# Attention and mixture of experts in one program: q and k in two float16 parts, two heads on the array's two 64-row halves

## The reference

```python
qkv = x @ W_qkv                               # (16,1024,256) @ (256,768)
q, k, v = split(qkv); q, k = rope(q, k)       # 16 heads of 16
att = einsum('bhtd,bhsd->bhts', q, k) / 4 + causal_mask
w = softmax(att)
x = layernorm(x + einsum('bhts,bhsd->bhtd', w, v) @ W_o)
gate = softmax(x @ Wg + bg); top 2 of 8, normalised
y = sum over experts of gate_e * (x @ We[e].T + be[e])
out = layernorm(x + y)
```

## Time and profile before

| | |
|---|---|
| three runs, median | 3236.32 us (3235.18 to 3238.13) |
| span of the profiled execution | 3236.3 us |
| PE busy | 3109.0 us, 96% of the span |
| DVE busy | 2677.5 us, 83% |
| ACT busy | 1884.1 us, 58% |
| POOL busy | 1200.8 us, 37% |
| chain that ended last | PE 84%, DVE 8%, issue 3%, ACT 2% |

### The profile page before, as it was taken

One profiled execution on the slowest core, in us unless ns is written; L12 is line 12 of the kernel. 1 busy time (PEld: TensorE's weight loads), 2 busy tenths in 40 slices (PEclk: granted clock), 3 DMA queues, 4 the chain that ended last, 5 costly groups with the idle time before them and its releaser, 6 DMA issues.

```text
span 3236.3 us, 58547 instructions
## 1 busy us (share of the span) xinstructions
PE 3109.0 (96%) x18752; PEld 1711.5 (53%) x18752; DVE 2677.5 (83%) x8452; ACT 1884.1 (58%) x4253; POOL 1200.8 (37%) x1414
## 2 busy tenths in 40 slices
PE   5789999999999999999999999999999999999987
PEld 2234555555555555555555555555555555555555
DVE  7687888888888888888888888888888888888745
ACT  2456556565655657556565655656565565755651
POOL 3253424343243443424344342434334244442110
PEclk8799999999999999999999999999999999999997
DMA  6344424433432433444233443433443243344000
GB/s 143 58 70 76 65 60 72 65 68 66 83 60 55 80 59 71 63 81 65 48 79 59 79 64 67 67 62 68 66 83 60 59 76 62 68 65 69 3 27 14
DMA packets 174819, 210.95 MB, mean 65 GB/s; under 512 B 26008, under 2 KB 124592, under 8 KB 174256
## 3 DMA queue, kind: packets, MB, share of 16 engines
q1 hardware_dynamic: 173056, 202.98, 36.1%
q10 hardware_dynamic: 1456, 4.23, 0.4%
HBM read 138.44 MB, written 67.11 MB: 64 GB/s over the span
## 4 chain that ended last, share of the span: by engine, by line
PE 84%; DVE 8%; issue 3%; ACT 2%; DMA 1%; POOL 1%; SPq 0%; ACTq 0%; DVEq 0%; POOLq 0%
PE bank L1052 23%; PE attend L1147 15%; PE scores L1125 14%; PE bank L1109 14%; PE bank L1089 6%; PE bank L1171 3%; PE bank L1098 3%; DVE bank L902 2%; PE bank L1155 1%; PE bank L1077 1%; PE bank L1162 1%; PE bank L1179 1%; DVE maxima L905 1%; PE bank L1203 1%; PE bank L1188 1%
## 5 line engine op out<-in xcount | busy, mean ns | idle before, releaser
L778 ACT ACTIVATE weights<-scores 128x512 f32<-128x512 f32 (+3 forms) x3072 | 1333.1, 494 | 926.0 <-PE scores L1125 913.5
L902 DVE CUSTOM_DVE_ANT_0 bank<-bank,far_q 128x128 f32<-128x128 f32 (+3 forms) x2048 | 962.9, 512 | 202.4 <-PE bank L1109 186.0
L1125 PE MATMUL scores<-q_stack,k_stack 99*128 99x512 bf16 (+3 forms) x3072 | 822.1, 329 | 16.6 <-DMA q_stack<-lowrows 7.3
L1109 PE MATMUL bank<-k_stack,q_stack 96*128 96x512 bf16 (+3 forms) x3072 | 799.5, 332 | 26.3 <-DMA k_stack<-parts_scratch 8.3
L692 POOL TENSOR_SCALAR_AFFINE_SELECT weights<-weights 128x512 f32<-128x512 f32 x512 | 325.5, 637 | 1253.5 <-ACT weights L778 1253.3
L905 DVE TENSOR_REDUCE maxima<-bank 128x1 f32<-128x512 f32 x1024 | 644.1, 682 | 72.6 <-PE bank L1109 72.4
L1147 PE MATMUL attend<-weights,values 128*32 128x512 f32 (+3 forms) x6144 | 583.0, 494 | 1.4 <-POOL weights L692 1.0
L1125 PEld LDWEIGHTS scores<-q_stack,k_stack 99*128 99x128 bf16 x3072 | 279.8, 97 | 417.8 <-ACT weights L778 151.6
L1109 PEld LDWEIGHTS bank<-k_stack,q_stack 96*128 96x128 bf16 x3072 | 276.7, 98 | 398.5 <-issue 166.4
L1052 PE MATMUL bank<-wexp_hi,zT_hi 128*128 128x512 f32 x1024 | 382.2, 454 | 11.1 <-DVE lowrows L922 11.1
L1026 DVE SCALAR_TENSOR_TENSOR z<-bank,picked,z 128x256 f32<-128x256 f32 x512 | 247.6, 484 | 114.6 <-PE bank L1052 105.6
(11 more groups left out here) (115 smaller groups left out, 3133.3 us busy)
## 6 DMA issues: line engine op xcount, KB each, us to landing
parts_scratch<-parts SPq DMA_DIRECT2D x128, 384.0 KB, 2.5
q_stack<-parts_scratch SPq DMA_DIRECT2D x384, 128.0 KB, 7.2
k_stack<-parts_scratch SPq DMA_DIRECT2D x384, 128.0 KB, 7.8
x_in<-in_x SPq DMA_DIRECT2D x64, 256.0 KB, 3.6
z<-in_x SPq DMA_DIRECT2D x32, 512.0 KB, 4.6
out<-z SPq DMA_DIRECT2D x32, 512.0 KB, 3.1
q_stack<-lowrows SPq DMA_DIRECT2D x192, 8.0 KB, 2.4
z<-in_w_exp ACTq DMA_DIRECT2D x1, 1024.0 KB, 5.1
```

The lines of the kernel that those rows point to most:

```text
L778: act.activation(weights[:, n % NW, hh, c0:CH], st[(QUAD * n + hh) % NS][:, c0:CH], ACT.Exp, scale=DH ** -0.5).then_inc(S["weights_ready"], 1)
L902: dve.tensor_tensor_reduce(out=b[:, 0:w], in0=b[:, 0:w], in1=far_q[:, CH - w:CH], scale=1.0, scalar=-SENTINEL, op0=ALU.add, op1=ALU.max, a ...
L1109: pe.matmul(b[:, 0:w], q_stack[0:ROWS, n, hh, qt * P:(qt + 1) * P], k_stack[0:ROWS, n, hh, kc * CH:kc * CH + w], start=True, stop=True).th ...
L1125: pe.matmul(st[(QUAD * n + hh) % NS][:, c0:CH], k_stack[0:MROWS, s, hh, kb * P:(kb + 1) * P], q_stack[0:MROWS, s, hh, qc * CH + c0:(qc + 1 ...
```

## The change

Four things change together.
- q and k are split into two float16 parts instead of three bfloat16 parts, with three terms instead of six: 48 rows instead of 96, and 51 with the maximum. One `CAST` per half remains instead of two.
- Two heads of a slot lie one above the other in the stacks, at partitions 0 and 64. `B` and `ST` read one or the other (`pair`), so the matmuls of an even and an odd head use different 64-row halves of the array. The tables now place the steps `.0 .1` and `.2 .3` next to one another everywhere.
- The maximum is split in three float16 steps of sizes 2^15, 2^5 and 1; a table `max_step` holds the factors, the split takes four operations on DVE as before, `LOAD` has 12 DMAs of half the size, and `MT` has 6 DMAs instead of 3.
- The tables MIDDLE and LAST are written anew: `MT.3` from row 2 to row 4, `MT.2` from row 38 to row 46, `LOAD.0` from row 4 to row 1, `LOAD.3` from row 37 to row 44, and most `MASK`, `PV` and `MOE` steps in other places. EARLY and FIRST are regrouped into pairs.

```diff
-TERMS = ((0, 0), (0, 1), (1, 0), (1, 1), (0, 2), (2, 0))
+TERMS = ((0, 0), (0, 1), (1, 0))
+NPART = 2
 ROWS = len(TERMS) * DH
+MAX_STEPS = (2.0 ** 15, 2.0 ** 5, 1.0)
+MROWS = ROWS + len(MAX_STEPS)
+PAIRS = 2
+HALF_ROWS = P // PAIRS
...
+        def pair(stack, rows, n, hh, cols):
+
+            base = HALF_ROWS * (hh % PAIRS)
+            return stack[base:base + rows, n, hh // PAIRS, cols]
...
-                    pe.matmul(b[:, 0:w], q_stack[0:ROWS, n, hh, qt * P:(qt + 1) * P],
-                              k_stack[0:ROWS, n, hh, kc * CH:kc * CH + w], start=True, stop=True).then_inc(fu, 1)
+                    pe.matmul(b[:, 0:w], pair(q_stack, ROWS, n, hh, slice(qt * P, (qt + 1) * P)),
+                              pair(k_stack, ROWS, n, hh, slice(kc * CH, kc * CH + w)), start=True, stop=True) \
+                        .then_inc(fu, 1)
...
-                    for part in range(3):
-                        dst = q_stack[ROWS + part:ROWS + part + 1, n, :, :]
-                        sp.dma_start(dst.rearrange("o h (t q) -> o (h t) q", q=P), maxrow[:, part, :]) \
-                          .then_inc(S[f"maxrow{n}"], DMA)
+                    for part in range(len(MAX_STEPS)):
+                        for i in range(PAIRS):
+                            row = HALF_ROWS * i + ROWS + part
+                            dst = q_stack[row:row + 1, n, :, :]
+                            src = maxrow[i * QUAD * TILES // PAIRS:(i + 1) * QUAD * TILES // PAIRS, part, :]
+                            sp.dma_start(dst.rearrange("o h (t q) -> o (h t) q", q=P), src) \
+                              .then_inc(S[f"maxrow{n}"], DMA)
...
-                    s, k, n = a
-                    if n:
-                        act.wait_ge(S["rest_ready"], c.at("rest_ready", ("CAST", s, k, 0)))
-                    else:
-                        act.wait_ge(S["rotated"], c.at("rotated", ("ROPE", s, k)))
...
+                    s, k = a
+                    act.wait_ge(S["rotated"], c.at("rotated", ("ROPE", s, k)))
...
+                    act.activation(parts[:, k % 2, 0], half_of(c, s, k), ACT.Copy).then_inc(S["cast"], 1)
```

The head and the tail of MIDDLE, before and after:

```diff
-XL.0 XL.1 XT.0 XL.2 XT.1 XL.3 B.0.0.0 B.0.0.1 MC.3
-ST.0.0 ST.0.1 B.0.0.2 B.0.0.3 B.0.1.0 B.0.1.1 ST.0.2 ST.0.3 MASK.0 B.0.1.2 PV.46 PV.47 YE.3.1 B.0.1.3
...
-ST.38.0 ST.38.1 MOE.1.2.1 ST.38.2 ST.38.3 B.3.2.1 B.3.2.2 MT.2 MASK.38 PV.36 PV.37
...
+XL.0 B.0.0.0 B.0.0.1
+ST.0.0 ST.0.1 PV.46 B.0.0.2 B.0.0.3 ST.0.2 ST.0.3 XL.1 B.0.1.0 B.0.1.1 PV.47 YE.3.1 B.0.1.2 B.0.1.3 XT.0 B.0.2.0
+  B.0.2.1
+ST.1.0 ST.1.1 XR.1 YT.3.1 B.0.2.2 B.0.2.3 VCOPY.3 MC.3 ST.1.2 ST.1.3 XT.1 XR.0 LOAD.0 MASK.0
+ST.2.0 ST.2.1 B.0.3.0 B.0.3.1 PV.0 ST.2.2 ST.2.3 B.0.3.2 B.0.3.3 XL.2 MASK.2 QK.0.0 MASK.1
+ST.3.0 ST.3.1 B.0.4.0 B.0.4.1 XT.2 ST.3.2 ST.3.3 B.0.4.2 B.0.4.3 MASK.3 PV.1 XL.3
...
+ST.44.0 ST.44.1 B.3.7.0 B.3.7.1 LOAD.3 VP.1 R2.1 B.3.7.2 B.3.7.3 MC.2 ST.44.2 ST.44.3 PV.42 B.3.8.0 B.3.8.1
+ST.45.0 ST.45.1 B.3.8.2 B.3.8.3 PV.43 B.3.9.0 B.3.9.1 MASK.44 ST.45.2 ST.45.3 N2A.1 B.3.9.2 B.3.9.3 PV.44
+ST.46.0 ST.46.1 B.3.10.0 B.3.10.1 MT.2 MASK.45 VP.2 B.3.10.2 B.3.10.3 ST.46.2 ST.46.3 YT.3.0 B.3.11.0 B.3.11.1
+ST.47.0 ST.47.1 VP.3 B.3.11.2 B.3.11.3 ST.47.2 ST.47.3 MASK.46 PV.45 MASK.47
```

More of the change, by code:

```diff
@@ L130 @@
[L130 to L143, removed]
@@ new lines @@
+ST.28.0 ST.28.1 GL.1 MASK.27 ST.28.2 ST.28.3 YT.1.1 PV.26 B.3.0.0 B.3.0.1
+ST.29.0 ST.29.1 PV.27 YE.2.0 B.3.0.2 B.3.0.3 GLT.1 ST.29.2 ST.29.3 GA.1 QK.1.2 ROPE.1.1
+ST.30.0 ST.30.1 GB.1 PV.28 B.2.5.0 B.2.5.1 ST.30.2 ST.30.3 B.3.1.0 B.3.1.1 PV.29
+ST.31.0 ST.31.1 PV.30 ST.31.2 ST.31.3 B.2.5.2 B.2.5.3 GT.1
+ST.32.0 ST.32.1 B.2.6.0 B.2.6.1 PV.31 B.3.1.2 B.3.1.3 ST.32.2 ST.32.3 BE.1.0 BE.1.1 YT.2.0 MOE.1.0.0 B.3.2.0
+  B.3.2.1
+ST.33.0 ST.33.1 MASK.32 MOE.1.0.1 ST.33.2 ST.33.3 B.2.6.2 B.2.6.3 MOE.1.0.2
@@ L267 @@
[L267 to L276 removed]
+B.0.0.0 B.0.0.1
@@ new lines @@
+ST.24.0 ST.24.1 MASK.23 PV.22 PV.23 B.1.11.0 B.1.11.1 ST.24.2 ST.24.3 MOE.0.3.0 B.1.11.2 B.1.11.3
+ST.25.0 ST.25.1 MOE.0.3.1 MOE.0.3.2 YE.1.1 ST.25.2 ST.25.3 MOE.0.3.3 MASK.24
+ST.26.0 ST.26.1 MC.1 MASK.25 ST.26.2 ST.26.3 PV.24 MASK.26
+ST.27.0 ST.27.1 ZT.1.0 ZT.1.1 ST.27.2 ST.27.3 MT.1 PV.25
+ST.28.0 ST.28.1 GL.1 MASK.27 ST.28.2 ST.28.3 YT.1.1 PV.26
+ST.29.0 ST.29.1 PV.27 YE.2.0 GLT.1 ST.29.2 ST.29.3 GA.1
+ST.30.0 ST.30.1 GB.1 PV.28 ST.30.2 ST.30.3 PV.29
+ST.31.0 ST.31.1 PV.30 ST.31.2 ST.31.3 GT.1
@@ L664, in _ @@
                                pattern=[[-1, P]], channel_multiplier=1).then_inc(S["const_p"], 1)
+            pool.memset(max_step[:, :], -MAX_STEPS[0]).then_inc(S["stepped"], 1)
+            for n, (row, size) in enumerate((HALF_ROWS * i + ROWS + part, MAX_STEPS[part]) for i in range(PAIRS)
+                                            for part in (1, 2)):
+                pool.wait_ge(S["stepped"], n + 1)
+                pool.affine_select(out=max_step[:, :], in_=max_step[:, :], compare_op=ALU.not_equal, fill=-size, base=-row,
+                                   pattern=[[1, 1]], channel_multiplier=1).then_inc(S["stepped"], 1)
+            pool.wait_ge(S["stepped"], 2 * PAIRS + 1)
             no_weight = pool.to_reg(0.0)
@@ L857, in _ @@
             dve.memset(taken[:, :, :], SENTINEL).then_inc(S["const_v"], 1)
-            dve.memset(k_stack[ROWS:MROWS, :, :, :], -1.0).then_inc(S["const_v"], 1)
             dve.wait_ge(S["const_p"], CONST_P)
+            for i in range(PAIRS):
+                rows = slice(HALF_ROWS * i + 32, HALF_ROWS * (i + 1))
+                last = k_stack[rows].rearrange("p s h t -> p (s h t)")
+                dve.tensor_copy(last, max_step[rows, 0:1].to_broadcast([32, SLOTS * QUAD // PAIRS * T])) \
+                   .then_inc(S["const_v"], 1)
             dve.wait_ge(S["ident_ready"], 1)
```

386 lines of the change are left out of this document (187 added, 199 removed).

## The result

The changed kernel takes 3199.94 us (median of 4, 3198.11 to 3213.09) against 3237.23 for the one before beside it; the ratio is 0.9895, 95% interval 0.9875 to 0.9916. It is 1% faster: clear of noise, but less than 2%. The forecast was 3063, and the range ended at 3145: the gain is 37 us where 173 were forecast.

A forecast was written before the change was run, and what follows sets the result against it. The prediction took a turn (191.9 us) to be bound by PE, with DVE 27 us behind. 14 turns at 181.2 us save 150, "last" 5, "pre" to "first" 18: 3236.3 becomes 3063 us; range 2960 to 3145.

The forecast's parts named there:

- Part 1: B and ST in the turns: two heads' matmuls run together on separate row halves, -29.5 us a turn.
- Rival 3: Every B and ST: the pairs run one after the other, 210 us a turn, 3487 us in all; chance 0.05.
- Part 2: PE in the turns: 150 more changes of the array's shape at 0.10 us each, +15.0 us a turn.
- the prediction's list of signs: What the profile after should show, including 0.3 us, not 0.2, between a pair of 512 columns and an MOE.
- Rival 1: Turns: shape changes are cheap and DVE becomes the bound, 171 us a turn, 2920 us in all; chance 0.12.
- Part 3: Turns: waits of the new order add 3.3 us (bounds 0 and 8), DVE none on average; a turn takes 181.2.
- the row sums: Larger of PE, DVE and ACT added over each three table rows: 191.3 us a turn old, 177.3 new.
- (b): Head of a turn: SP issues XL.2 only behind LOAD.0, so XT.2 waits 1.3 us.
- (a): Head of a turn: MT.2 is too close ahead of ST.0.0, which waits 2 us with all of PE's queue.
- rival 2: Turns: DVE and PE wait for each other more, head waits reach 8 us; 187 a turn, 3150 us; chance 0.12.
- Part 4: The ends: "last" gains 5 us, and "pre" to "first" gains 18 through shorter loads and fewer passes.
- rival 4: The clock falls: a tenth of the turns at 1.2 GHz would give 3335 us; chance 0.03.

The follow-up runs named there:

- e1: Changed kernel with scores and row maxima reading all 128 rows, so no pairs run together and no shape changes around them; output meaningless: 3305.08 us.
- e2: Changed kernel with both heads of a pair reading the lower half's rows, so a pair's matmuls run one after the other; shape changes stay: 3561.65 us.
- e7: Changed kernel with ROPE.0.2 and ROPE.1.1 moved behind GT.0 and GT.1 in the middle order: 3191.78 us.
- e5: Changed kernel with row maxima taken over 128 columns of each tile instead of up to 512, so VectorE has less work: 3112.94 us.
- e9: Changed kernel with XL.2 and XL.3 both ahead of LOAD.0 in the middle order: 3178.24 us.
- e13: Changed kernel with row maxima over 128 columns, XL.2 and XL.3 ahead of LOAD.0, and ROPE.0.2 and ROPE.1.1 behind GT: 3057.77 us.

## Why the prediction was wrong, step by step

**Part 1, two heads side by side: right.** The second of a pair starts 0.003 us after the first (median of the records in the turns), and the next matmul 0.226 us after a pair of 512 columns. That fewer rows make no matmul shorter is also borne out: one of 512 columns takes 0.216 us in e1 on 128 rows and 0.216 to 0.226 in e2 on 48 or 51. Own time from e2 to the changed kernel: -30.8 us, forecast -29.5. Rival 3, the pairs one after the other, fell; e2 is what it would have been, 2939.0 / 14 = 209.9 us a turn (forecast 210).

**Part 2, changes of the array's shape: right in kind, too small.** The count, 58 and 208 changes, was right, and from a pair of 512 columns to MOE it is 0.31 us, as the prediction's list of signs had it. By own time the trips into whole-array work cost 16.4 us and the added PV stretches 2.6 (186.5 to 189.1): +19.0 (17.6 by the coarser grouping), where +15.0 was forecast and 18 was the bound. By the turns the trips cost 12.6, which would make the sum look right (15.4 with 2.8 for the PVs), but e1's longer waits are in that. Not seen: the price has a third piece, the block's first matmul, so that a trip costs 0.29 around MOE or QK and 0.24 around four transposes, where two changes were taken at 0.20. Rival 1, cheap changes, fell.

**Part 3, the waits: the step that failed.** Own time fell by 11.8 us (186.5 to 174.7: +19.0 less 30.8), where the row sums gave 14; that is 2.2 us a turn of the miss. Above it, +3.3 was forecast and +9.0 came (5.5 to 14.5): 5.7 us, the larger part. "DVE therefore adds nothing on average" was wrong: adding up the larger of PE, DVE and ACT over three rows of the table takes it that a bank is always free to hold what DVE is behind with. Two pairs fill all four banks. DVE is busy 2366.3 of 2641.3 us (90%), within what the forecast allowed (88 to 93%), but it is late at single places: B waits for it 118 times in the run, 47.5 us. That the four banks are why is argued from these waits; no run varied their number. "DVE's work stays" was not quite right either: it is 169.0 us a turn instead of 164.7, and with POOL's rotation moved away (e7) 164.0. e5 took 4.0 us a turn off by VectorE alone, e9 1.1 by x_in alone (2625.9 / 14 = 187.6), e13 8.0 with VectorE, x_in and GT. The Trainium skill says on "TensorEngine Tiling (Array Packing)", under PSUM Bottleneck, that after a fourfold speedup of TensorE the copy out of PSUM may become the bottleneck. Here the speedup is twofold, and on B and ST alone; the trace goes the same way, by 47.5 us of waits for banks against 10.2, but with PE still leading the chain (71%, DVE 15%). Of the two waits at the head, (b) was right and a little too small (1.6 us a turn ahead of XT.2 against 1.3), (a), forecast at 2 us, did not come in the changed kernel; it comes, with 0.2 to 1.5 us, once VectorE is relieved (e5, e13). Its rows of 4 KB land in 1.7 us instead of the 2.4 that I took; the rest of that chain was not taken apart. One wait was in no step: VectorE's small operations for the gates run beside POOL's rotation and hold GT (21.9 us against 8.4). This was rival 2 (turn 187, chance 0.12) in what it says of DVE and PE, and nearly in size, 188.7; the waits at the head, which it put at 8 us, stayed under 2.

**Part 4, the ends: wrong by 32 us.** "Pre" to "first" gained 6.2 us ahead of "early", as much as one load, and lost 14.4 in "first", where -18 in all was forecast. There the granted clock is 0.79 instead of 0.97. This is rival 4 in one stage: e1, the same order without halves, has 0.97 and 151.6 us; e2, with halves and PE busy 168 of 184, has 0.72 and 183.8. So PE's waits are not what lowers the clock there. The argument against the rival, "0.97 with PE busy at only 86%", was drawn from whole-array work. Whether it is the rows or the changes of shape was not separated, nor how much of the 14.4 us is the clock's: PE's busy time in "first" is 8.9 us up (129.2 to 138.1) and its idle time 5.5. e1 has the new order without halves and 151.6 us, so at most 1.6 are the order's. "Last" stayed (+0.6, forecast -5), and "post" gave 2.9.

**The sum.** Profiled span 3196.4 less 3063: 14 x 7.5 = 105 from the turns, 26 from "pre" to "first", 5.6 from "last", -2.9 from "post". The range was too narrow at the upper end: it ended below rival 2's own 3150, and rival 2 and rival 4 were taken as exclusive, where each came in part and their losses add up.

## What to carry to other kernels

When an engine that leads is made faster, its own time can be forecast from rows to 2% of a turn (which was still a fifth of the change in it), but what lies above it can't be taken over from the trace before: count what the next engine is behind with at each place against the buffers between them, above all when that engine is nearly full, as VectorE was here (86% before, 90% after). A written-out order belongs to the durations that it was written for: with the old parts the new order was 11% slower, and bringing blocks together to save shape changes, some 40 us by expectation, cost 114. A wait that is removed at one place of a busy queue comes back at the next one (XT.2 to XT.3 behind SP's loads, GT to B behind VectorE), so remove all of them before judging one.
